# Degree products moved earlier in a pipelined scatter, and a control table read two turns at a time

## The reference, cut to what matters

```python
h    = relu(layernorm(x)) @ W_in + b_in
deg  = segment_sum(ones(E), row=src, N)
dis  = where(deg > 0, rsqrt(max(deg, 1)), 0)
for _ in range(3):
    cur = segment_sum(cur[col] * (dis[row] * dis[col])[:, None], row, N)   # col = dst
    acc = acc + cur
x    = x + (acc / 4) @ W_out + b_out
```

## Time and profile before

| | us |
|---|---|
| median of 3 runs (974.76 to 976.95) | 975.67 |
| the profiled execution | 974.94 |
| its span, first to last instruction | 973.4 |
| TensorE matmuls busy | 787.6 |
| VectorE busy | 710.2 |
| GpSimd busy | 487.2 |
| ScalarE busy | 355.6 |
| mean granted TensorE clock | 0.941 |

### The profile page before, as it was taken

How to read it: one execution, slowest core, us unless ns; L and a number is a source line. 1 busy time by engine, 2 the same in 40 slices (tenths; PEclk the granted TensorE clock), 3 DMA queues, 4 the chain that set the end, 5 groups by cost and what they waited for, 6 DMA issues and landing times.

```text
span 973.4 us, 27338 instructions
## 1 busy us (share of the span) xinstructions
PE 787.6 (81%) x5974; PEld 584.6 (60%) x5975; DVE 710.2 (73%) x2380; ACT 355.6 (37%) x705; POOL 487.2 (50%) x609
## 2 busy tenths in 40 slices
PE   6577667667879999997189889898888888887877
PEld 4254333334549999996067667666666666655545
DVE  7999999997635645346077677776778877887885
ACT  1424668998740000013054444433433332222100
POOL 2145433420018300101577777777777777777772
PEclk9699999998659999998589999999999999999999
DMA  4024456994320000114932121211212222221213
GB/s 124 24 81 104 124 145 152 161 167 115 95 68 2 1 1 2 34 55 116 324 85 54 51 54 52 53 52 52 54 51 54 52 54 51 53 53 52 53 52 88
DMA packets 64856, 73.33 MB, mean 75 GB/s; under 512 B 12805, under 2 KB 53180, under 8 KB 64670
## 3 DMA queue, kind: packets, MB, share of 16 engines
q1 hardware_dynamic: 48366, 37.31, 15.5%
q0 software_dynamic: 16432, 35.29, 14.4%
HBM read 43.85 MB, written 8.22 MB: 53 GB/s over the span
## 4 chain that ended last, share of the span: by engine, by line
PE 33%; DVE 25%; issue 15%; DVEq 10%; POOL 8%; DMA 5%; ACT 2%; SPq 1%; POOLq 0%; ACTq 0%
PE ps L1198 15%; PE ps L1275 9%; POOL CT L662 8%; DVE ohbuf L829 6%; DVE CT L972 5%; PE ps L1106 4%; DMA CT<-h_dram,src_col 4%; DVE CT L975 3%; DVEq L975 3%; DVE u L829 3%; DVEq L128 3%; PE ps L1254 2%; DVEq L972 2%; DVE ohbuf L824 1%; ACT stage L1355 1%
## 5 line engine op out<-in xcount | busy, mean ns | idle before, releaser
L662 POOL DMA_INDIRECT CT<-h_dram,src_col x391 | 370.3, 947 | 125.1 <-issue 102.5
L1275 PE MATMUL ps<-CT 128*128 128x256 f32 x1180 | 303.1, 405 | 64.4 <-DVE CT L972 31.3
L1275 PEld LDWEIGHTS ps<-CT 128*128 128x128 f32 x1180 | 202.8, 191 | 158.9 <-issue 142.2
L975 DVE SCALAR_TENSOR_TENSOR CT<-ps,dlP,CT 128x256 f32<-128x256 f32 x580 | 279.7, 482 | 4.3
L972 DVE COPY CT<-CT 128x128 f32 x590 | 148.4, 252 | 124.5 <-PE ps L1275 57.9
L1417 ACT COPY CT<-ps 128x256 f32<-128x256 f32 x200 | 77.6, 388 | 306.3 <-PE ps L1275 302.6
L1106 PE MATMUL ps<-ohbuf 128*128 128x400 bf16 x395 | 104.8, 374 | 37.4 <-DVE ohbuf L829 14.8
L1198 PE MATMUL ps<-u,CT 128*128 128x192 bf16 x1250 | 105.0, 246 | 1.7 <-DVEq L937 0.9
L1355 ACT CAST stage<-ps 128x800 bf16<-128x800 f32 x100 | 82.3, 823 | 63.5 <-PE ps L1106 62.5
L1198 PEld LDWEIGHTS ps<-u,CT 128*128 128x128 bf16 x1250 | 103.0, 98 | 2.9 <-DVEq L901 1.3
L1254 PE MATMUL ps<-CT 128*128 x800 | 95.8, 277 | 6.8 <-ACT CT L1417 4.6
(11 more groups left out here) (184 smaller groups left out, 647.6 us busy)
## 6 DMA issues: line engine op xcount, KB each, us to landing
CT<-stage SPq DMA_DIRECT2D x200, 100.0 KB, 3.5
u<-types_dram POOLq DMA_DIRECT2D x49, 128.0 KB, 3.5
CT<-h_dram,src_col POOLq DMA_INDIRECT x391, 2.5
coef_dram<-coef_out POOLq DMA_DIRECT2D x49, 64.0 KB, 4.0
CT<-coef_dram SPq DMA_DIRECT2D x1, 3048.0 KB, 12.0
out<-CT SPq DMA_DIRECT2D x4, 256.0 KB
ohbuf<-x SPq DMA_DIRECT2D x3, 320.0 KB, 3.8
x_dram<-ohbuf SPq DMA_DIRECT2D x3, 320.0 KB, 2.4
```

Source lines behind the costliest of these rows:

```text
L662: pool.indirect_dma_start(out=gring[:, (j + 1) % GRING, :], out_offset=None, in_=h2_dram, in_offset=bass.IndirectOffsetOnAxis(ap=src_col[: ...
L975: dve.scalar_tensor_tensor(kpair[:, u, :, :], nodes.unsqueeze(1).broadcast_to([P, BASES, WIN]), dl, coef_flat[:, ds(tiles * -BASES + NT * ...
L1275: pe.matmul(ps[:, ds(summed.place(counts[u][0], RING), 1), 0:WIN * BASES], gpair[:, u, :], kpair[:, u, :, :].rearrange("p b d -> p (b d)") ...
```

## The change

The packed table loses its two unused words per turn (ROW = 2), so the words of two turns lie side by side. The TensorE loop ends earlier: it covers turns 19 to 39 (`DEG_FROM` = 391 // 10 + 2 = 41, `looped` = 13 passes counted from turn 1). The clearing product follows it, and turns 40 to 58 are written out. In these turns one load at each even turn brings the words of that turn and the next (four registers; at turn 58 two), and odd turns load nothing. The degree products are dealt out over turns 41 to 58: after turn c as many are done in all as `ready` = (c - 40) * 23 // 18 says, which is 1, 2, 3, 5, 6, 7, 8, 10 after turns 41 to 48, and 11, 12, 14, 15, 16, 17, 19, 20, 21, 23 after turns 49 to 58. Two groups (k = 23 and 24) stay behind the last turn. The number of products, their operands and their waits are the same.

```diff
-ROW = 4
+ROW = 2
...
+DEG_FROM = NT // U + 2
...
-            count_words = [pe.alloc_register(f"count_word{i}") for i in range(2)]
+            count_words = [pe.alloc_register(f"count_word{i}") for i in range(4)]
...
-            def count_pairs(c, phase, coefs=True):
-                pe.load(count_words, tab_count[0:1, slice(c, c + 1) if isinstance(c, int) else ds(c, 1), 0:2]
-                        .rearrange("p c i -> p (c i)"))
+            def count_pairs(c, phase, coefs=True, pair=None):
+                if pair is None:
+                    pe.load(count_words[0:2], tab_count[0:1, slice(c, c + 1) if isinstance(c, int) else ds(c, 1), :]
+                            .rearrange("p c i -> p (c i)"))
+                elif not pair:
+                    n = min(2, TURNS - c)
+                    pe.load(count_words[0:2 * n], tab_count[0:1, c:c + n, :].rearrange("p c i -> p (c i)"))
+                words = count_words[2:4] if pair else count_words[0:2]
                 for u in range(U):
                     h = (2 * phase + u // HU) % HALVES
-                    word = count_words[u // HU]
+                    word = words[u // HU]
...
-            with pe.Fori(peeled, (CT_TURNS - 1) // HALVES) as q:
+            looped = (DEG_FROM - 1) // HALVES
+            with pe.Fori(peeled, looped) as q:
...
             pe.matmul(ps[:, 7, :], zb, zw, start=True, stop=True)
-            for c in range(CT_TURNS, TURNS):
-                count_pairs(c, c % HALVES, coefs=False)
-                assert (c - CT_TURNS + 1) * 2 * WPG <= c * U - NT
-                for k in range((c - CT_TURNS) * 2, (c - CT_TURNS + 1) * 2):
+            added = 0
+            assert looped * HALVES % 2 == 1
+            for c in range(1 + looped * HALVES, TURNS):
+                count_pairs(c, c % HALVES, coefs=c < CT_TURNS, pair=c % 2)
+                ready = max(c - DEG_FROM + 1, 0) * (NG - 2) // (TURNS - DEG_FROM)
+                assert ready * WPG <= max(c * U - NT, 0)
+                for k in range(added, ready):
                     add_degrees(k)
-            for k in range((TURNS - CT_TURNS) * 2, NG):
+                added = ready
+            for k in range(added, NG):
                 last = add_degrees(k)
             last.then_inc(deg_done, 1)
```

## The result

| | before | after |
|---|---|---|
| median, us | 975.49 (973.98 to 976.95, 7 runs) | 970.56 (967.53 to 973.55, 7 runs) |
| ratio to before | | 0.9952, 95% interval 0.9937 to 0.9967 |
| profiled execution, us | 974.94 | 967.53 |
| its span, us | 973.4 | 966.0 |

The change makes the kernel 4.9 us faster by the medians (the ratio gives 4.7, between 3.2 and 6.1); 4.5 were forecast. The profiled execution of the changed kernel is the fastest of its seven, 3.0 us under their median. Part of its lead lies outside the changed stages: it reaches turn 41 1.15 us earlier (192.34 against 193.49) and takes 0.9 us less behind the last degree product, with the same code there. The three changed stages together give 92.06 - 86.67 = 5.4 us. The fastest of the seven had a mean granted clock of 0.952, the slowest 0.939.

A forecast was written before the change was run, and what follows sets the result against it. TensorE was taken to bind turns 49 to 58, but not turns 41 to 48. +1.5 us in the first stretch and -6.0 in the second gave -4.5, 971.2 us for a median, with a range of 966.0 to 978.3.

The forecast's parts named there:

- The bound and the floor: Turns 49 to 58 are bound by TensorE; ScalarE's pace sets a floor of 42.4 us, 9.7 us less than now.
- Part 1: Ten blocks of 25 degree products move into turns 41 to 48: +1.5 us, between 0 and +5.5.
- Part 2: Turns 49 to 58 run 11 blocks instead of 18: seven blocks of 0.70 us, 4.9 us less TensorE work.
- Part 3: One load for two turns: four gaps of 0.43 us go in turns 49 to 58, 1.7 us, between 0 and 2.2.
- The sum: Whole kernel: +1.5 - 6.0 = -4.5 us, 970.4 for the profiled execution, 971.2 for a median.
- Part 4: The tail behind turn 58: fewer blocks there gain nothing, the 8.18 us stay.
- the fetch: Turns 40 to 48 fetched as straight code: taken as 0; as a rival +1.5 to +3 us, 978, chance 0.05.
- The clock drops from turn 41 on and stays down: Rival: +5.5 us in turns 41 to 48, -4 or so in 49 to 58, net +1.5 to +2.5, 977.7; chance 0.16.
- the mark of 36 us: Sign: turns 41 to 48 taking above 36 us means the clock falls there and stays down; 31.8 to 34 was forecast.
- The ring takes over: Rival: TensorE's shorter turns become waits for ScalarE's zeros and VectorE's buffers; -3.3 us there, -1.5 net, 974.2; chance 0.18.
- The full gain: Rival: the clock stays up and ScalarE is fed at its pace: -8 to -9.7 us, 966 to 967.5; chance 0.13.

The follow-up runs named there:

- no_degrees: The changed kernel without the degree products of groups 0 to 23, only those of group 24 run: 965.96 us, ratio 0.9905 to the kernel before.
- deal_only: The changed kernel with one load of two words in every turn, as before, the degree products dealt over turns 41 to 58: 974.46 us, ratio 0.9975.
- sum_two: The changed kernel, with TensorE's table of sums in the relational layer loaded for two turns at once, four aligned words: 967.69 us, ratio 0.9919.
- after_wide: The changed kernel with each degree product 20 columns wide instead of one: 967.63 us, ratio 0.991 to the kernel before.
- loads_even: The kernel before with one load for two turns, pairs beginning at even turns, degree products left in place: 971.11 us, ratio 0.9957.
- unroll_only: The kernel before with turns 40 to 48 written out instead of looped, nothing else changed: 975.88 us, ratio 1.0003.
- loads_only: The kernel before with one load for two turns, pairs beginning at odd turns, degree products left in place: 975.19 us, ratio 0.9998.
- four_each: The changed kernel, but every turn from 40 to 57 loads four words and uses its own two: 979.53 us, ratio 1.0039 to the kernel before.
- four_words: The changed kernel, with all other table loads of TensorE bringing four registers instead of two, at odd and even turns: 984.38 us, ratio 1.0087.
- run 11: Experiment 11, sum_two: the changed kernel with the relational layer's table of sums loaded for two turns at once: 967.69 us, ratio 0.9919.

## Why the prediction was right, point by point

**The bound and the floor: right.** Turns 49 to 58 were bound by TensorE and have a floor at ScalarE's pace: 42.4 us forecast, 42.51 in no_degrees, where ScalarE's casts wait 0.6 us for products instead of 10.6.

**Part 1, blocks into turns 41 to 48: the mechanism right, the size too small.** Forecast +1.5 us between 0 and +5.5. The profile after has +2.8; deal_only's +5.8, with a clock of 0.82; sum_two's, of the same code as the change, +6.4 at 0.73; after_wide's +4.5. These are single executions, but all lie above the term. Without the ten blocks the stretch took 31.6 to 33.0 us in six executions, so the price is some 4 us. TensorE's idle time in it shrank by 4.2 us (10.1 to 5.9), where I had written some 7. The slack of TensorE at full clock (29.0 us of work in 31.77) was thus not enough; how the price divides over clock and ring wasn't measured. The cost of a block itself was right: 250 products in 7.4 us are 0.74 a block, not the estimated 2.7 us that the section LDWEIGHTS of the Trainium skill's "TensorE: Matmul & The Clock Gate" would give. The trace shows how both can be: one weight load's own record is 96 ns long, close to the page's figure, but the loads run over one another, 250 of them in 7.1 us.

**Part 2, seven blocks out of turns 49 to 58: rather over-valued.** Parts 1 and 2 together should give -4.9 + 1.5 = -3.4 us. Alone, the dealing gave -2.4 (deal_only), with an interval of 0.8 to 4.1 that holds the forecast; its turns 49 to 58 took 2.7 us less than before. On top of the loads at even turns it gave -0.5, which the two intervals, 0.9943 to 0.9971 and 0.9937 to 0.9967, can't tell from nothing.

**Part 3, the loads: under-valued, and this is the weakest step.** I took 1.7 us with 2.2 as the bound, and wrote "That one load now brings four words I cost at nothing". Alone, loads_even gave -4.2; with the dealing in place the loads are still worth 0.9975 - 0.9952, 2.2 us, which can't be told from 1.7. Three things are in the 4.2: four gaps of 0.43 go, as forecast; each load left is 0.2 us shorter, which the rows showed on another engine and I read as a difference of the engines; and the clock is up longer (0.79 against 0.66), presumably because the wide products follow one another more closely. The last I had named as possible and priced at nothing. How the 4.2 us divide over the three wasn't measured.

**The sum was right partly by luck.** In the two profiles of the changed code turns 49 to 58 take 7.6 and 7.7 us less than before, where 6.0 was forecast, and turns 41 to 48 take 2.8 and 6.4 more, where 1.5 was: a gain and a price that were both put too low. Parts 2 and 3 draw on one reserve, the 9.6 us between 52.1 and ScalarE's floor of 42.5. Their runs gave -2.4 and -4.2 alone and -4.7 together, not -6.6; but the intervals leave the missing 1.9 us open (some 2.7 either way), so that the gains don't add up is likely and not shown.

**Part 4 and the fetch: right.** The tail moved by 0.6 us where 0 was forecast; code fetch costs nothing that shows (unroll_only, 1.5 us slower at most).

**The rivals.** "The clock drops from turn 41 on and stays down" didn't come in the measured median, but its first half is real: sum_two's profile of the same code passes the mark of 36 us that the prediction had set for it (38.18, clock 0.73), though turns 49 to 58 then take 44.37 and not 47 to 48.5. The fastest run of the changed kernel has the highest clock of the seven (0.952) and the slowest, 6.0 us above it, one of the lowest (0.939). "The ring takes over" (its -3.3 is half of parts 2 and 3 together, not of part 2 as written) isn't what held the gain down: TensorE waits 6.7 us in turns 49 to 58 for its two neighbours, but it waited 7.8 before, and after_wide, with the same ring, gets 8.8 us. "The full gain" of 8 to 9.7 us needs the clock; after_wide has it.

## What to carry to other kernels

Before moving work off a bound engine, look at what stands between its pieces: here halving the 0.4 us gap behind some blocks and closing it behind others gave 4.2 us, while moving seven blocks of work gave 2.4 (the intervals overlap), and the clock rose with the first. When two edits aim at one stretch, find its floor from the next engine's pace and don't add their gains beyond it. If an engine's clock falls in a stretch of very thin products, try wider ones before you move or remove them: 20 columns instead of one gave nearly what leaving 600 products out gave. And an experiment that undoes one part must keep the others' hidden conditions: the first trial of the loads began 8 bytes off and said that the part is worth nothing. And before pricing an edit in a stage, look for what goes through it at a constant pace: 391 gathers in 488 us, the same in every kernel, say in one line that shorter loads can gain little there.

## What the runs showed of the hardware

- A register load on TensorE takes 0.54 us for two words, in rows of 16 bytes (the kernel before) and of 8 (turns 0 to 39 after) alike. For four it mostly takes 0.33 to 0.34 us if the first lies on a multiple of 16 bytes from the table's start (even turns, sum_two) and 1.0 to 1.6 us if it lies 8 bytes behind one (loads_only, odd turns of four_each and four_words). So four aligned words come faster than two.
- Products of 20 columns with their weight loads take the time of products of one column, 28 ns each at half clock, and in turns 49 to 58 the granted clock is 0.86 to 0.94 with them (three executions), against 0.65 and 0.66 before and 0.76 and 0.79 after the change without. With no degree products there it is 0.84.
- A gather of source rows on GpSimd takes 0.94 us, and one starts each 1.25 us, in every kernel here.
- Over the queue for instructions ten blocks of 16 KB came between 190 and 290 us beside CT's transfers (0.9% of the engines' time; seven in the kernel before). Written-out turns alone, in unroll_only, cost nothing that can be measured:

```profile
q8 instruction: 10, 0.16, 0.9%
```
